# First pass: the first layer with its folded taps by high and low parts, each blended block split on POOL

## The chip, the cores and the metric

One core of one Trainium2 chip runs the whole kernel. The metric is the device time of one execution in microseconds; the time before is the median of three runs. TensorE is the matrix engine (PE in the rows, its weight loads PEld), VectorE is DVE, ScalarE is ACT, GpSimd is POOL, and SyncE (SP) issues most transfers.

## The reference

The input is x, 32 images of 56 x 56 positions with 96 channels, fp32. Four layers follow one another (L0 to L3). Only the first, L0, is touched here:

```python
x_norm = (x - mu) / sqrt(var + EPS) * gamma + beta
x_gray = x_norm.mean(-1)
grad_h = abs(x_gray[:, :, 1:] - x_gray[:, :, :-1]).mean(axis=(1, 2))
grad_v = abs(x_gray[:, 1:, :] - x_gray[:, :-1, :]).mean(axis=(1, 2))
scores = stack([grad_h, grad_v, 0.8 * (grad_h + grad_v) * 0.5, abs(grad_h - grad_v)], axis=1)
idx = argmax(softmax(relu(scores @ sel_w1 + sel_b1) @ sel_w2 + sel_b2), axis=-1) % 4
x_sel = where(idx == 1, swapaxes(x_norm, 1, 2), x_norm)
t = x_sel.reshape(b, h * w, c) @ fc1_w + fc1_b
t = depthwise_convolution_of_3_along_the_sequence(t, dw_w) + dw_b
out = gelu(t) @ fc2_w + fc2_b
return x + out
```

L1 to L3 are blocks of windowed attention with an MLP or a convolution; their code is the same before and after.

## The kernel before

`scan_pass` computes L0; three calls of `window_pass` compute L1 to L3 after it. In `scan_pass` an image lies in SBUF as 96 channels by 3136 positions, cut into NB = 7 blocks of TB = 448 positions. Each engine has its own program, written out by hand, and semaphores order them.

`step(i, norm, conv, turn)` runs three things side by side on each engine: normalising image i and deciding its flag (norm), the convolution and the second layer of image i - 1 (conv), and transposing image i + 1 (turn). `over_images` calls it for image 0, then in a loop for images 1 to 30, then for 31, and last for the convolutions of image 31 alone. A step has 14 slots k = 0 to 13, one for each half block: block m = k // 2, half h = k % 2 of the 192 hidden channels.

- TensorE. `conv_half` (L395) computes half a block of the first layer: the three taps of the convolution are folded into the weights `W1T`, so it is three fp32 matmuls of 97 rows, 96 columns of weights and 448 positions, on `XS` shifted by 0, 1 and 2 positions, added up in one bank. `fc2_block` (L407) is the second layer of a block, `mean` (L373) and `variance` (L379) serve the normalisation, `turn_block` (L359) transposes. The small matmuls of the decision stand ahead of their slots: score (L433, slot 9), sel1 (L436, slot 10), sel2 (L439, slot 11), flag (L442, slot 12). `conv_half` waits, at the first half of a block, until the blended blocks up to m + 1 are there (`xs`), and for the Gelu that frees its bank.
- ACT. Squares (L473), Ln and Exp for the reciprocal deviation (L481, L484), Gelu (L511). Gelu and Ln/Exp are in different table sets, so a table load stands between them.
- VectorE. Copies of the turned image out of PSUM (L531), centring copies `XM` (L565), the product `XN` (L570), the small operations of the decision (L584 to L612), the residual into `OUT` (L543, two instructions, which read the bank and `XM`), and the blend: for each block `XS = XN * (1 - flag)` (L620) and `XS = XN transposed * flag + XS` (L623). The blend stands in slots 12 (blocks 0 to 2) and 13 (blocks 3 to 6), with the residual of block 5 between them and that of block 6 behind, and then the centring copy of the next image.
- SP loads images and stores `OUT`. POOL has nothing to do in this pass.

`XS` has two buffers, taken in turn by images, and a row of ones for the bias (L258). The helper `split_weights` (L153, L157) is used for the later passes: on VectorE it makes `high = cast(whole)` in fp32r and `low = whole - high`. There, `by_parts` (L998) and `output` (L1090) compute a product as high x high + high x low + low x high with three fp32r matmuls, and POOL splits operands (L1473 and L1475, L1482 and L1484, L1535 and L1537).

Of the kernel before, what the change touches and what calls it, by code (L numbers as in the profile page):

```python
# [31 lines left out]
F32R = mybir.dt.float32r  # L32
# [157 lines left out]
def scan_pass(nc, PS, w, x, xa):  # L190
# [20 lines left out]
    with ExitStack() as ctx:  # L211
# [10 lines left out]
        XT = sb("XT", [112, TP, C]); X = sb("X", [C, S])  # L222
        XM = sb("XM", [GY, 2, S]); XN = sb("XN", [GY, S]); XS = sb("XS", [C + 1, 2, S + 2])
        SQ = sb("SQ", [C, 2, 2 * TB]); LV = sb("LV", [GY, 2, 2 * TB]); RS = sb("RS", [GY, 2, 2 * TB])
# [22 lines left out]
        with nc.Block() as block:  # L247
            @block.tensor
            def _(pe):
                pe.matmul(PS[0:C, 1, 0:1], J[:, 0:C], gcol[:, 0:1], start=True, stop=True).then_inc(gamma_mean, 1)  # L250

            @block.vector
            def _(dve):
                for t in range(3):
                    dve.tensor_tensor(W1T[0:C + 1, t, :], W1[0:C + 1, :], taps[0:C + 1, t, :], ALU.mult)

                for p in range(2):
                    dve.memset(XS[C:C + 1, p, 1:S + 1], 1.0)  # L258


                dve.tensor_tensor(CM[:, 0:C], ident[0:C, 0:C], J[:, 0:C], ALU.subtract)
                dve.wait_ge(gamma_mean, 1)
                dve.tensor_copy(gmean[:], PS[0:C, 1, 0:1]).then_inc(gamma_out, 1)
                dve.wait_ge(gamma_out, 1)
                dve.tensor_scalar(CM[:, C + 1:C + 2], gcol[:], gmean[:, 0:1], 1.0 / C, ALU.subtract, ALU.mult)

        s = {n: sem(n) for n in ("img_loaded", "turned", "x_ready", "mean", "xm", "sq", "var", "lv", "rstd",
                                 "xn", "grey_tiles", "diffs", "sums", "sums_ready", "score", "scores", "sel1", "hidden", "sel2",
                                 "dve_chain", "centred", "expo", "flag", "flagb", "flag_ready", "factors", "blend", "xs",
                                 "conv", "gelu", "fc2", "out")}  # L270
        stored, passed = [sem("stored0"), sem("stored1")], sem("passed")
# [28 lines left out]
        with nc.Block() as block:  # L300
# [49 lines left out]
            def _(pe):  # L350
# [30 lines left out]

                def conv_half(c, xs, k):

                    m, h = k // 2, k % 2
                    if h == 0:

                        pe.wait_ge(s["xs"], c * NB + min(m + 2, NB))
                    if k >= 3:
# [5 lines left out]
                    for t in range(3):  # L394
                        mm = pe.matmul(PS[0:C, 4 + k % 3, 0:TB], W1T[0:C + 1, t, h * C:(h + 1) * C],  # L395
                                       xs[:, m * TB + t:m * TB + t + TB], start=(t == 0), stop=(t == 2))
                    mm.then_inc(s["conv"], 1)
# [12 lines left out]
                def step(i, norm, conv, turn):  # L410
                    c = base(pe, i - 1)
                    i1 = base(pe, i + 1)
                    xs = pick(XS, parity(pe, c)) if conv else None
                    for k in range(SLOTS):
# [28 lines left out]
                        if conv:  # L443
                            conv_half(c, xs, k)
                            if k % 2 == 1 and k >= 3:
                                fc2_block(c, k // 2 - 1)
# [75 lines left out]
            def _(dve):  # L522
# [23 lines left out]
                def step(i, norm, conv, turn):  # L546
# [11 lines left out]
                    if norm:  # L558
                        p = parity(dve, i)
                        xm, xs = pick(XM, p), pick(XS, p)  # L560
                    old = pick(XM, parity(dve, c)) if conv else None

# [9 lines left out]
                    for k in range(SLOTS):  # L572
# [43 lines left out]
                        if norm and k >= FLAG:  # L616

                            for m in (range(NB // 2), range(NB // 2, NB))[k - FLAG]:
                                cols = slice(1 + m * TB, 1 + (m + 1) * TB)
# [11 lines left out]
                for m in range(NB):  # L631
                    copy_turned(0, m)
                over_images(dve, step)


# [1111 lines left out]
```

## Time and profile before

| | |
|---|---|
| time, median of 3 runs | 11815.78 us (11811.32 to 11822.69) |
| profiled execution, its own time | 11807.14 us |
| its span, first to last instruction | 11805.3 us |
| mean granted TensorE clock | 0.977 |
| PE busy | 11116.6 us (94%) |
| DVE busy | 7378.2 us (62%) |
| ACT busy | 7831.3 us (66%) |
| POOL busy | 5227.8 us (44%), none of it in the first pass |
| L395 PE, first layer of the first pass | 2688 records, 552 ns on average |

All times in the rows are from that one profiled execution. In the first pass one image follows another in the same pattern, so the rows of one image (from 1012 to 1077 us) stand for the pass. A fp32 matmul shows as two records of the matmul and two weight loads; an fp32r matmul shows as one of each. Matmul records overlap, so the distance between starts is what one costs.

### The profile page before, as it was taken

How to read it: one execution, taken by the hardware profiler on the slowest of the kernel's cores; microseconds unless marked ns; L12 is line 12 of the kernel's file. 1: busy time of each engine (PE TensorE's matmuls, PEld its weight loads, DVE VectorE, ACT ScalarE, POOL GpSimd, SP SyncE). 2: the span in 40 equal slices, each digit the busy share in tenths (PEclk: the TensorE clock that was granted, in tenths of full speed). 3: DMA queues.
4: the chain of work that ended last, by engine and by line, in shares of the span. 5: the costliest groups of instructions: out<-in, count | busy, mean ns of one | idle time of the engine just before them, and what ended most of it. 6: DMA issues, size and time to landing. Idle time of an engine off the chain costs nothing. (4 is left out here: it accounts for less than half of the span.)

```text
span 11805.3 us, 397033 instructions
## 1 busy us (share of the span) xinstructions
PE 11116.6 (94%) x158740; PEld 8317.4 (70%) x158740; DVE 7378.2 (62%) x12642; ACT 7831.3 (66%) x13524; POOL 5227.8 (44%) x6916
## 2 busy tenths in 40 slices
PE   6999999899999999998989999998999999999999
PEld 2444444577777777777767777776888888788887
DVE  4444444577777777775447777776666666666665
ACT  4555555477777777776337777775777777777776
POOL 0000000377777777775014544443555555555554
PEclk9999999899999999999989999998999999999999
DMA  1111111122222222222643333332010000010100
GB/s 54 39 40 36 40 35 40 33 53 50 52 51 51 51 52 51 51 51 77 216 146 80 81 79 79 80 79 54 24 25 24 25 24 24 25 25 25 24 24 22
DMA packets 1105622, 617.63 MB, mean 52 GB/s; under 512 B 864651, under 2 KB 1076566, under 8 KB 1099704
## 3 DMA queue, kind: packets, MB, share of 16 engines
q1 hardware_dynamic: 1091496, 553.66, 19.3%
q10 hardware_dynamic: 12288, 38.54, 1.0%
q8 instruction: 1265, 20.73, 0.8%
q14 instruction: 573, 4.69, 0.1%
HBM read 308.38 MB, written 282.75 MB: 50 GB/s over the span
## 5 line engine op out<-in xcount | busy, mean ns | idle before, releaser
L1484 POOL TENSOR_TENSOR L_HdL<-L_Hd,L_HdH 128x392 fp32r<-128x392 f32 x1536 | 1572.7, 1024 | 283.8 <-POOL L_HdH L1482 283.1
L1468 POOL TENSOR_TENSOR L_SQ<-L_X 96x392 f32<-96x392 f32 x512 | 428.5, 837 | 2298.8 <-DMA L_X<-after_L 2288.6
L991 PE MATMUL banks<-L_ident,L_PR 113*113 113x113 f32 x9216 | 1201.1, 267 | 1.2 <-DVE L_X L1390 0.7
L991 PEld LDWEIGHTS banks<-L_ident,L_PR 113*113 113x113 f32 x9216 | 1143.1, 180 | 63.8 <-DVE L_X L1390 9.8
L1219 ACT COPY L_PT<-banks 113x452 f32<-113x452 f32 x1792 | 885.8, 538 | 371.1 <-PE banks L991 369.2
L1235 ACT ACTIVATE L_PR<-L_SX 113x588 f32<-113x588 f32 x1536 | 1088.0, 708 | 52.3 <-DVE L_SX L1362 10.3
L1482 POOL CAST L_HdH<-L_Hd 128x392 fp32r<-128x392 f32 x1536 | 785.1, 511 | 740.5 <-issue 658.1
L395 PE MATMUL banks<-scan_XS,scan_W1T 97*96 (+1 forms) x2688 | 1111.4, 552 | 0.0
L1054 PE MATMUL banks<-L_VB,L_PT 113*49 113x34 f32 x36864 | 1064.1, 213 | 2.0 <-ACT L_PT L1219 1.0
L1262 ACT ACT_TABLE_LOAD x512 | 656.9, 1283 | 607.3 <-PE banks L998 607.2
L1356 DVE TENSOR_REDUCE L_MX<-banks 113x12 f32<-113x588 f32 x1024 | 783.4, 765 | 432.2 <-PE banks L1037 432.2
L1054 PEld LDWEIGHTS banks<-L_VB,L_PT 113*49 113x49 f32 x36864 | 1016.1, 126 | 25.4 <-issue 2.5
L1473 POOL CAST L_XNH<-L_XN 97x392 fp32r<-97x392 f32 x512 | 447.6, 874 | 1155.4 <-DVE L_XN L1403 1155.4
L1362 DVE TENSOR_TENSOR L_SX<-banks,L_MX 113x588 f32<-113x588 f32 x1024 | 788.9, 770 | 35.3
L395 PEld LDWEIGHTS banks<-scan_XS,scan_W1T 97*96 97x96 f32 x2688 | 434.0, 167 | 514.9 <-issue 510.6
L1037 PEld LDWEIGHTS banks<-L_KX,L_QT 32*49 32x49 f32 x36864 | 562.6, 118 | 310.0 <-issue 307.9
L1037 PE MATMUL banks<-L_KX,L_QT 32*49 32x98 f32 x36864 | 720.3, 248 | 28.9 <-issue 28.0
L1090 PE MATMUL banks<-L_HdH,L_W2H 128*97 128x392 f32 x1536 | 611.1, 398 | 130.4 <-POOL L_HdL L1484 130.2
L1013 PE MATMUL banks<-L_Wv,L_XN 97*49 97x48 f32 x24576 | 730.2, 213 | 0.0
L1532 POOL COPY L_XN<-L_XR 96x392 f32<-96x392 f32 x256 | 147.9, 578 | 1276.5 <-DMA L_XR<-L_norm 1270.7
L1371 DVE COPY L_PT<-banks 113x452 f32<-113x452 f32 x512 | 321.9, 629 | 617.9 <-PE banks L991 617.9
L1072 PE MATMUL banks<-L_OT,L_Wp 97*97 97x392 f32 x1536 | 691.9, 532 | 2.8 <-ACT L_OT L1265 1.1
(239 smaller groups left out, 27006.6 us busy)
## 6 DMA issues: line engine op xcount, KB each, us to landing
L_X<-after_L SPq DMA_DIRECT2D x768, 147.0 KB
after_L<-L_X SPq DMA_DIRECT2D x512, 147.0 KB
conv_T<-L_norm_by_phase SPq DMA_DIRECT2D x96, 512.0 KB, 3.3
L_norm_by_phase<-L_XP SPq DMA_DIRECT2D x512, 84.0 KB, 2.1
scan_XT<-in_x SPq DMA_DIRECT2D x33, 1176.0 KB, 7.1
L_norm<-L_XA SPq DMA_DIRECT2D x256, 147.0 KB, 1.9
L_conv<-conv_D ACTq DMA_DIRECT2D x96, 392.0 KB, 3.0
L_XR<-L_norm SPq DMA_DIRECT2D x256, 147.0 KB, 2.6
```

The lines of the kernel that those rows point to most:

```text
L395: mm = pe.matmul(PS[0:C, 4 + k % 3, 0:TB], W1T[0:C + 1, t, h * C:(h + 1) * C], xs[:, m * TB + t:m * TB + t + TB], start=(t == 0), stop=(t ...
L991: mm = pe.transpose(bank(TURN[a])[0:SPAN, (k % 4) * SPAN:(k % 4 + 1) * SPAN], PR[:, st.v if lag else st.u, 2 * k:2 * k + 2, :].rearrange(" ...
L1013: mm = pe.matmul(bank(VALUES_BANK)[HALF * e:HALF * e + TOK, q * G * HD:(q + 1) * G * HD], XN[:, st.u, q * TOK:(q + 1) * TOK], Wv[0:C + 1, ...
L1037: mm = pe.matmul(bank(g)[p0:p0 + TOK, q // 2 * 2 * TOK:(q // 2 + 1) * 2 * TOK].rearrange("c (e k) -> c e k", e=2), QT[rows, st.u, q * TOK: ...
L1054: mm = pe.matmul(bank(HEADS_BANK)[p0:p0 + TOK, col:col + VW], PT[:, st.v, q // 2 * G + g, p0:p0 + TOK], VB[:, st.v, q, g, :], start=True, ...
L1072: pe.matmul(bank(PROJ_BANK)[0:C + 1, 0:CH], Wp[0:C + 1, :], OT[:, st.v], start=mlp, stop=True).then_inc(s["proj"], 1)
L1219: act.copy(PT[:, st.v if lag else st.u, 4 * a:4 * a + 4, :].rearrange("c k q -> c (k q)"), bank(TURN[a])[0:SPAN, 0:4 * SPAN]).then_inc(s[f ...
L1235: act.activation(PR[:, u, a, 0:TOK], SX[:, u, a], ACT.Exp).then_inc(s[f"probs{half}"], 1)
L1356: dve.tensor_reduce(mx, src, AX.X, ALU.max).then_inc(s[f"rowmax{half}"], 1)
L1362: dve.tensor_tensor(dst, src, spread, ALU.subtract).then_inc(s[f"centred{half}"], 1)
L1482: pool.tensor_copy(HdH[:, u, j].bitcast(F32R), Hd[:, u, j]).then_inc(s[f"hd_high_{j}"], 1)
L1484: pool.tensor_tensor(HdL[:, u, j].bitcast(F32R), Hd[:, u, j], HdH[:, u, j], ALU.subtract).then_inc(s[f"hd_parts_{j}"], 1)
```

## The change

The first layer of the first pass is computed by high and low parts. `W1T` is split once into `W1TH` and `W1TL` with `split_weights`, which also splits the prepared `XS` (zero edges, row of ones) into both buffers of `XSH` and `XSL`. For each image VectorE blends into a single buffer `XS`; POOL casts each blended block to fp32r (`XSH`) and subtracts (`XSL`), and raises `xs_parts`, for which `conv_half` now waits. `conv_half` issues nine fp32r matmuls in place of three fp32 ones. VectorE waits for `xs_parts` of the image before ahead of the first blend.

```diff
-        XM = sb("XM", [GY, 2, S]); XN = sb("XN", [GY, S]); XS = sb("XS", [C + 1, 2, S + 2])
+        XM = sb("XM", [GY, 2, S]); XN = sb("XN", [GY, S]); XS = sb("XS", [C + 1, S + 2])
+        XSH = sb("XSH", [C + 1, 2, S + 2]); XSL = sb("XSL", [C + 1, 2, S + 2])
+        W1TH = sb("W1TH", [128, 3, 2 * C]); W1TL = sb("W1TL", [128, 3, 2 * C])
...
-                for p in range(2):
-                    dve.memset(XS[C:C + 1, p, 1:S + 1], 1.0)
+                dve.memset(XS[C:C + 1, 1:S + 1], 1.0)
...
+        split_weights(nc, "scan_parts", [(W1T[0:C + 1], W1TH[0:C + 1], W1TL[0:C + 1])]
+                      + [(XS[:], XSH[:, p], XSL[:, p]) for p in range(2)])
...
-                def conv_half(c, xs, k):
+                def conv_half(c, xh, xl, k):
...
-                        pe.wait_ge(s["xs"], c * NB + min(m + 2, NB))
+                        pe.wait_ge(s["xs_parts"], c * NB + min(m + 2, NB))
...
-                        mm = pe.matmul(PS[0:C, 4 + k % 3, 0:TB], W1T[0:C + 1, t, h * C:(h + 1) * C],
-                                       xs[:, m * TB + t:m * TB + t + TB], start=(t == 0), stop=(t == 2))
+                        for n, (wt, xt) in enumerate(((W1TH, xh), (W1TH, xl), (W1TL, xh))):
+                            mm = pe.matmul(PS[0:C, 4 + k % 3, 0:TB], wt[0:C + 1, t, h * C:(h + 1) * C].bitcast(F32R),
+                                           xt[:, m * TB + t:m * TB + t + TB].bitcast(F32R), start=(t == 0 and n == 0), stop=(t == 2 and n == 2))
...
+                            if k == FLAG and (not isinstance(i, int) or i >= 1):
+                                dve.wait_ge(s["xs_parts"], i * NB)
...
+            @block.gpsimd
+            def _(pool):
+                def step(i, norm, conv, turn):
+                    if not norm:
+                        return
+                    p = parity(pool, i)
+                    xh, xl = pick(XSH, p), pick(XSL, p)
+                    for m in range(NB):
+                        cols = slice(1 + m * TB, 1 + (m + 1) * TB)
+                        hold(pool, s["xs"], i * NB + (m + 1), passed)
+                        pool.tensor_copy(xh[0:C, cols].bitcast(F32R), XS[0:C, cols]).then_inc(s["xs_high"], 1)
+                        hold(pool, s["xs_high"], i * NB + (m + 1), passed)
+                        pool.tensor_tensor(xl[0:C, cols].bitcast(F32R), XS[0:C, cols], xh[0:C, cols], ALU.subtract).then_inc(s["xs_parts"], 1)
+
+                over_images(pool, step)
```

## Rows read from the trace of the kernel before

**Rows 1.** The page, its first line: the span.

```profile
span 11805.3 us, 397033 instructions
```

**Rows 2.** Busy us of PE, PEld, DVE, ACT, POOL in a stretch; clock, DMA.

```profile
1056.00:1060.00 4.00, 4.00 (x15) 2.38 (x13) 3.82 (x7) 1.55 (x2) 0.00 (x0) 0.57 0.20 50
```

**Rows 3.** Timeline of PE, one image: start us, us, line, tiles, [idle <- releaser].

```profile
1012.68 4.75 PE L395 MATMUL banks<-scan_XS,scan_W1T 97*96 x12
1017.27 1.67 PE L407 MATMUL banks<-scan_Hd,scan_W 96*97 96x448 f32 x4
...
1029.90 1.75 PE L379 MATMUL banks<-scan_SQ,scan_J 96*98 96x448 f32 x4 [0.54 <-ACT scan_SQ L473]
...
1055.15 2.27 PE L359 MATMUL banks<-scan_ident,scan_XT 112*96 112x112 f32 x16 [1.69 <-ACT scan_LV L481]
1057.22 3.60 PE L395 MATMUL banks<-scan_XS,scan_W1T 97*96 x6
...
1066.27 0.18 PE L433 MATMUL banks<-scan_gone,scan_GA 56*4 56x1 f32 x2 [0.53 <-issue]
...
1072.91 0.19 PE L439 MATMUL banks<-scan_sw,scan_hid 16*1 16x4 f32 x2
...
1076.96 0.33 PE L442 MATMUL banks<-scan_fl,scan_one 1*96 1x2 f32 x2
```

**Rows 4.** Timeline of DVE, the same image.

```profile
1013.76 0.45 DVE L620 TENSOR_SCALAR scan_XS<-scan_XN,scan_fb 96x448 f32 x1 [0.16 <-DVE scan_fb L612]
...
1015.21 0.45 DVE L620 TENSOR_SCALAR scan_XS<-scan_XN,scan_fb 96x448 f32 x1
...
1019.17 0.81 DVE L543 SCALAR_TENSOR_TENSOR scan_OUT<-banks,scan_fc2b,scan_XM 97x424 f32<-97x424 f32 x2 [0.98 <-PE banks L407]
...
1024.69 1.04 DVE L623 SCALAR_TENSOR_TENSOR scan_XS<-scan_XN,scan_fb,scan_XS 96x448 f32 x1
...
1076.51 0.14 DVE L609 TENSOR_SCALAR scan_fl<-scan_fl 1x1 f32<-1x1 f32 x1
```

**Rows 5.** Timeline of ACT, the same image.

```profile
1027.60 1.28 ACT L473 ACT_TABLE_LOAD   x1 [9.51 <-DVE scan_XM L565]
```

**Rows 6.** Timeline of PE in the second pass: fp32r matmuls in a row.

```profile
3011.22 0.34 PE L998 MATMUL banks<-L_XNH,L_WqH 97*96 97x392 f32 x1
...
3011.40 0.34 PE L998 MATMUL banks<-L_XNL,L_WqH 97*96 97x392 f32 x1
```

**Rows 7.** Timeline of DVE and POOL in the second pass.

```profile
3005.73 0.57 DVE L1407 TENSOR_TENSOR L_XN2L<-L_XN,L_XN2H 97x392 fp32r<-97x392 f32 x1
3005.79 0.88 POOL L1473 CAST L_XNH<-L_XN 97x392 fp32r<-97x392 f32 x1 [1.17 <-DVE L_XN L1403]
```

**Rows 8.** Third pass, DVE and POOL: timeline, then groups (count, busy us, mean ns, idle).

```profile
6520.86 0.51 POOL L1535 CAST L_XNH<-L_XN 97x392 fp32r<-97x392 f32 x1 [0.17 <-POOL L_XN L1532]
6520.90 1.09 DVE L1362 TENSOR_TENSOR L_SX<-L_SR,L_MX 113x588 f32<-113x588 f32 x1
...
6521.55 1.32 POOL L1537 TENSOR_TENSOR L_XNL<-L_XN,L_XNH 97x392 fp32r<-97x392 f32 x1 [0.18 <-POOL L_XNH L1535]
...
L1545 POOL TENSOR_TENSOR L_DWL<-L_DW,L_DWH 96x392 fp32r<-96x392 f32 x256 | 260.3, 1017 | 46.1 <-POOL L_DWH L1543 46.1
...
L1362 DVE TENSOR_TENSOR L_SX<-banks,L_MX 113x588 f32<-113x588 f32 x1024 | 788.9, 770 | 35.3
```

**Rows 9.** Timeline of DVE while constants and weights are prepared.

```profile
56.05 2.67 DVE L258 MEMSET scan_XS<- 1x3136 f32 x1 [0.69 <-issue]
...
2188.38 0.21 DVE L153 CAST L_WqH<-L_Wq 97x96 fp32r<-97x96 f32 x1 [0.64 <-PEq L73]
...
2188.62 0.35 DVE L153 CAST L_W1H<-L_W 97x384 fp32r<-97x384 f32 x1
...
2189.23 0.26 DVE L157 TENSOR_TENSOR L_WqL<-L_Wq,L_WqH 97x96 fp32r<-97x96 f32 x1
...
2189.57 0.55 DVE L157 TENSOR_TENSOR L_W1L<-L_W,L_W1H 97x384 fp32r<-97x384 f32 x1
```

More of the change, by code:

```diff
@@ L269, in scan_pass @@
                                  "dve_chain", "centred", "expo", "flag", "flagb", "flag_ready", "factors", "blend", "xs",
-                                 "conv", "gelu", "fc2", "out")}
+                                 "xs_high", "xs_parts", "conv", "gelu", "fc2", "out")}
         stored, passed = [sem("stored0"), sem("stored1")], sem("passed")
@@ L412, in step @@
                     i1 = base(pe, i + 1)
-                    xs = pick(XS, parity(pe, c)) if conv else None
+                    if conv:
+                        p = parity(pe, c)
+                        xh, xl = pick(XSH, p), pick(XSL, p)
                     for k in range(SLOTS):
@@ L443, in step @@
                         if conv:
-                            conv_half(c, xs, k)
+                            conv_half(c, xh, xl, k)
                             if k % 2 == 1 and k >= 3:
@@ L559, in step @@
                         p = parity(dve, i)
-                        xm, xs = pick(XM, p), pick(XS, p)
+                        xm, xs = pick(XM, p), XS
                     old = pick(XM, parity(dve, c)) if conv else None
@@ L633, in _ @@
                 over_images(dve, step)
+            @block.gpsimd
[4 more added lines that the diff above has]
+                    p = parity(pool, i)
+                    xh, xl = pick(XSH, p), pick(XSL, p)
+                    for m in range(NB):
[5 more added lines that the diff above has]
+                over_images(pool, step)
 class Step:
```

## The prediction

> **What bounds the kernel now.** The page gives the profiled execution a span of 11805.3 us [rows 1]. The change touches the first pass alone. A busy share, 94% of the span for TensorE, is no bound, so I followed one image through the timeline of each engine, from L395 of slot 12 at 1012.68, which stands right behind the flag matmul, to the next flag matmul at 1076.96: 64.3 us, 64.5 with the flag matmul itself [rows 3]. It falls into four parts, and TensorE sets the end of only some.
>
> - S1, flag to the ACT table load ahead of the square (1027.60) [rows 5]. VectorE sets it: seven blends, the residual of block 5, the residual of block 6 and the centring copy. Its one wait is 0.98 us, for the second layer's matmuls [rows 4]; ACT then waited 9.51 us for that copy [rows 5], and TensorE 0.54 us for the square (L379) [rows 3].
> - S2, from there to the transposes at 1055.15: a chain of table loads, squares, Ln and Exp on ACT with the copies of VectorE in it. TensorE waits for it, 1.69 us at the transposes [rows 3]; convolutions 2 to 6 lie beside it.
> - S3, transposes to score matmul (1066.27): TensorE until the second layer of block 2, then VectorE's residual, its three copies L531 and the sums; at the score TensorE had idled 0.53 us [rows 3].
> - S4, score to flag: TensorE back to back; behind sel2 (1072.91) a parallel chain of softmax pieces whose last part L609 ends at 1076.65 [rows 4], 0.31 us ahead of the flag matmul.
>
> **The matmuls.** Half a block was 3 fp32 matmuls, 6 records; the 12 records of two halves take 4.59 us from 1012.68 to the next row's start at 1017.27, the first of them a little longer: 2.25 us a half, 0.375 a record [rows 3]. It becomes 9 fp32r matmuls. The nearest rows step 0.18 us at 392 columns [rows 6]; scaled by columns a step is between 0.195 (only the 56 extra columns at the rate of the fp32 pass, 0.375 / 448 / 2 each) and 0.21. I take 0.20, and 0.07 for the first of a group: 1.87 us, so 0.38 less a half. If the extra address arithmetic of 9 instructions showed, it would be near 2.1 and the saving 0.15; nothing below the 9 steps is possible.
>
> What that brings by part, without POOL. S1: two halves precede the residual that VectorE awaits, but its own blends end 0.98 us before: -0.76. S2: zero, ACT's chain covers it; if ACT were not there it would be 5 x 0.38. S3: convolution 7 runs partly at the lower clock level: its six records take 3.60 us, not 2.42, and the stretch 1056 to 1060 has a granted clock of 0.57, so most of it is at 1.2 instead of 2.4 GHz [rows 2, 3], behind a wait of 1.69 us and the transposes. The slow stretch is a stretch of time: in it an fp32 record steps 0.75, an fp32r one 0.375 (448 columns at half the rate), so it costs both about half its length. The gain stays near 0.38, a little more as a step of 0.20 less than doubles: -0.43. Convolution 8 gains nothing, the three copies are late next. S4: convolutions 9 and 10 give 0.38 each; for 11 the softmax chain is late next, so only 0.15: -0.91. Sum: -2.10 us an image.
>
> **The splits on POOL.** Each blended block now gets a cast and a subtraction on POOL, 96x448. Nearest rows: cast 0.51 us (L1535) and subtraction 1.02 (L1545) for 392 columns [rows 8]; scaled, 0.56 and 1.15, with a step of some 0.18 us between them and ahead of each. That is 2.0 us a block against VectorE's 1.45 (1013.76 to 1015.21) [rows 4]. POOL idles in this pass, and TensorE needs only two blocks' parts before convolution 0, ten microseconds later, so POOL's own time is hidden. VectorE's new wait (the parts of the image before) is long satisfied and costs nothing; queued behind it would be the blends.
>
> What is not hidden is the use of SBUF by both. In the second pass a POOL cast that met VectorE's subtraction with two SBUF inputs (L1407) took 0.88 us, not 0.51: it ended 0.37 us after VectorE's [rows 7]. In the third pass VectorE's L1362, SBUF inputs both, started 0.04 us after a POOL cast and took 1.09 us where the same shape takes 0.77: it ended 0.62 us after the cast. POOL's next operation then met L1362 and took 1.32 instead of 1.02 [rows 8]. So such operations exclude each other whole. L623 has two SBUF inputs (XN and XS). L620 has one, but moves 448 elements in 0.45 us: less than the 1.0 ns an element of a two-input operation (0.26 us at 96, 0.55 at 384, L157) and in line with the cast's 0.49 ns (0.21 and 0.35, L153) [rows 4, 9]: it uses two read paths, and no row shows such an operation against POOL.
>
> The Trainium skill, "SBUF — State Buffer", section "SBUF: two separate sides", says of the pair shared by VectorE and GpSimd that it is held by whichever starts first, for the whole instruction, and that a two-port mode takes it as well as two SBUF inputs. By that L620 excludes POOL too, and the sum would be the upper of the two below, 11918 us.
>
> Worked through from L620 at 1013.76, where a blocked operation runs its own time less 0.14 after the other's end (the L1362 and L1537 rows): L620 0.31, L623 0.91, cast 0.42, subtraction 1.00. If POOL is served at every hand-over, a block costs VectorE 0.31 + 0.42 + 0.91 + 1.00 = 2.64 us; the first two are freer, and the last blend ends at 1030.2, where it ended at 1025.7: +4.5. If VectorE keeps the pair from L623 to the next L620, POOL enters only in the gap ahead of L623, alternately with a cast and a subtraction: 1028.9, +3.2. The 0.98 us of waiting is used up in both. I take +3.8 between these ends, because the rows don't tell the order at a hand-over. This replaces S1's -0.76. Outside these ends lies the case without exclusion, a rival below.
>
> **The rest.** Setup: a new block before the loop, on VectorE and in series. Casts: 0.44 + 2 x 1.7; subtractions: 0.74 + 2 x 3.3 by the slopes above for 576 and 3138 columns; the barrier ahead of such a block 0.64 (the idle time before the first cast [rows 9]) and about as much behind it: 12.4. Off goes one memset of ones, 2.67 + 0.60 [rows 9]: +9.1. The smaller first memset lies under the loads. The last step has convolutions alone, TensorE back to back: 14 x 0.38 = -5.3.
>
> **Sum.** 31 x (3.8 - 0.91) = +89.6; 30 x (-0.43) = -12.9; +9.1 - 5.3: +80.5 us. On the span of 11805.3 us that is 11885.8; the execution's own time is 1.8 more than its span (11807.14), and the median of the runs, 11815.78, is 8.6 more than that: 11896.
>
> **The rivals.**
> - Exclusion at its two ends (both in my forecast): +3.2 gives 11878, +4.5 gives 11918.
> - L620 doesn't exclude POOL. Then POOL gets in under it and L623 waits only for the rest: the last blend ends at 1026.1, +0.35. 31 x (0.35 - 0.91) - 12.9 + 3.8 = -26: 11789. For it: no row shows a one-input operation blocked. Against: its rate of two elements in the time of one.
> - No exclusion: 31 x (-0.76 - 0.91) - 12.9 + 3.8 = -61: 11755, faster. It decides if the rows of the passes with POOL were due to something else; three kinds of row say otherwise.
> - More idle, lower clock: TensorE now waits 5 to 6 us for the square in each image where it waited 0.54. If the clock falls there, variance 0 ends up to 1.7 us later; ACT reads it only behind two table loads (1.28 us each [rows 5]), two Gelus and a square, so that is free; but a second fall over convolutions 9 to 11 would add 1 to 2 us an image, beside the exclusion: 11927 to 11958.
> - The splits' parts arrive late for the convolutions: POOL would have to need over 5 us a block (convolution time of a block with its second layer); at 2.6 it doesn't decide.
>
> **How the numbers follow.** Exclusion, either order, 0.66: 11855 to 11935 with the matmul step and the clock of convolution 7 open. Worse (clock, or POOL slower than its rows) 0.10. Partial exclusion 0.13. None 0.11. About 0.2%, 24 us, is what a measurement of this kernel can tell. Partial exclusion spreads over both sides of that line, half and half. Faster 0.18, same 0.08, slower 0.74. The range takes in the partial case at 11775 and part of the worse one to 11942; the forecast's own range is 11855 to 11935.
>
> **What would show each step.** L395: nine fp32r records a half, step 0.20. L623 and L620: means over 1.05 and 0.45, L623 near 1.3 to 1.9; POOL's casts over 0.56. From flag to the table load about 19 us, from the table load to the transposes 27.5 as before; L379 waiting about 5 us for the square; score to flag 9.8. If L620 and L623 keep their means, the prediction is wrong and the time falls under 11800; if the step of L395 is 0.24 or more, the gains of S3 and S4 vanish and it goes to 11925 or over.

## The result and the profile after

| | before | after |
|---|---|---|
| median of the runs (15 each), us | 11814.59 | 11844.65 |
| ratio, 95% interval | 1 | 1.0026 (1.0017 to 1.0034) |
| the profiled execution, us | 11807.14 | 11852.66 |
| its span, us | 11805.3 | 11850.9 |

The change makes the kernel 30 us slower by the medians; the two profiled executions are 45.6 us apart by their spans. Two of the 15 runs of after, 12341 and 12827 us at a granted clock of 0.80 and 0.75 where the others have 0.97, stay out of the ratio; without them the median of after is 11842.77 us. Here are the span and the busy times on the page of after, to be held against [rows 1]:

```profile
span 11850.9 us, 401791 instructions
PE 11020.4 (93%) x160084; PEld 8592.4 (73%) x160084; DVE 7502.6 (63%) x12647; ACT 7843.1 (66%) x13524; POOL 5678.7 (48%) x7364
```

TensorE is less busy than before and the kernel is slower: the busy share was no bound. The first thing to do is to cut both spans at the memset of the PSUM banks that opens each pass. The cut gives, in us:

| pass | before | after | difference |
|---|---|---|---|
| 1 (changed) | 2164.4 | 2222.3 | +57.9 |
| 2 | 3923.4 | 3903.8 | -19.6 |
| 3 | 2083.0 | 2085.0 | +2.0 |
| 4 | 3634.5 | 3639.7 | +5.2 |

Passes 2 to 4 compute the same by the same code, and the second is 20 us shorter. The forecast had nothing there.

The first pass, by the parts of the prediction, as means over the 24 images between the 6th and the 30th flag (us; the first two columns count from the flag matmul). The table counts S1 to the square itself; the prediction counted it to the table load ahead of the square, which starts 1.29 us earlier in both kernels, so the differences are the same:

| | last blend ends | square starts (S1) | square to transposes (S2) | transposes to score (S3) | score to flag (S4) | flag to flag |
|---|---|---|---|---|---|---|
| before | 13.32 | 16.48 | 26.25 | 10.77 | 10.67 | 64.17 |
| after | 15.72 | 18.88 | 26.28 | 10.79 | 9.68 | 65.63 |
| difference | +2.40 | +2.40 | +0.03 | +0.02 | -0.99 | +1.46 |

Now the lines. Timeline of DVE of after, blocks of the blend (start, us, engine, line, operation, out<-in); [rows 4] are the same work before:

```profile
1046.60 0.45 DVE L628 TENSOR_SCALAR scan_XS<-scan_XN,scan_fb 96x448 f32<-96x448 f32 x1
...
1048.55 1.25 DVE L631 SCALAR_TENSOR_TENSOR scan_XS<-scan_XN,scan_fb,scan_XS 96x448 f32<-96x448 f32 x1
...
1058.12 1.17 DVE L631 SCALAR_TENSOR_TENSOR scan_XS<-scan_XN,scan_fb,scan_XS 96x448 f32<-96x448 f32 x1
1059.21 1.27 DVE L628 TENSOR_SCALAR scan_XS<-scan_XN,scan_fb 96x448 f32<-96x448 f32 x1
1060.52 1.14 DVE L631 SCALAR_TENSOR_TENSOR scan_XS<-scan_XN,scan_fb,scan_XS 96x448 f32<-96x448 f32 x1
```

The same stretch on POOL; the bracket is the idle time before a line and who ended it:

```profile
1048.47 0.56 POOL L653 CAST scan_XSH<-scan_XS 96x448 f32 x1 [50.12 <-DVE scan_XS L631]
...
1058.75 1.49 POOL L655 TENSOR_TENSOR scan_XSL<-scan_XS,scan_XSH 96x448 f32 x1 [0.24 <-POOL scan_XSH L653]
1060.18 0.72 POOL L653 CAST scan_XSH<-scan_XS 96x448 f32 x1
...
1062.58 0.56 POOL L653 CAST scan_XSH<-scan_XS 96x448 f32 x1
```

Read the ends. L631 ends at 1059.29. The subtraction, which POOL had begun at 1058.75, ends at 1060.24, 0.95 us later, so it did most of its work behind L631. L628, begun at 1059.21, ends at 1060.48, 0.24 us behind the subtraction: alone it takes 0.45 (the line at 1046.60), here 1.27. The cast begun at 1060.18 ends at 1060.90, 0.42 us behind L628. L631, begun at 1060.52 with 0.38 us of the cast to go, ends at 1061.66, 0.76 us behind the cast. So each waits for the other's end, as the forecast had it, and a block takes 0.95 + 0.24 + 0.42 + 0.76 = 2.37 us, where it took 1.45.

The last of the four waits is easily overlooked, because L631 grows by only 0.10 us, from 1.04 to 1.14. It is a wait all the same. The cast begun at 1048.47 ends at 1049.03; L631, begun at 1048.55 with 0.48 us of it to go, takes 1.25 and ends at 1049.80, 0.77 us behind it. Between 200 and 2000 us there are 165 such meetings of L631 with a cast, and it ends 0.75 to 0.79 us behind the cast in all of them, 0.77 in the mean. L631 grows by what is left of the cast when it starts, less 0.28 us.

This is one image of two kinds. In every second image, which uses the other of the two buffers, the subtraction takes 1.31 us and not 1.47, and a block 2.21 us; the mean of the blocks from the third on is 2.30. POOL's operations grow too, the cast from 0.56 to 0.72 us and the subtraction from 1.13 (0.97 in the other buffer): that is the same exclusion seen from the other side.

What follows from the late copy is in the waits of TensorE, 1000 to 1900 us (what waited, for what: us in total, times, longest), first before, then after:

```profile
PE banks L359 <- ACT scan_LV L481: 23.6, 14, 1.7
PE banks L379 <- ACT scan_SQ L473: 20.4, 28, 0.9
```

```profile
PE banks L382 <- ACT scan_SQ L479: 57.9, 28, 4.4
PE banks L362 <- ACT scan_LV L487: 35.8, 14, 2.6
```

L382 (was L379) now waits up to 4.4 us for the square, since the matmuls are shorter and the square later. Those are the idle microseconds that the fp32r matmuls freed; they are not on the path.

### The profile page after: what moved, and what is told of

Read it like the earlier page. It is cut to its first block and busy times, and to the rows that moved or that the text cites. A ratio compares the mean times of both kernels' runs of the same rounds, so it can differ in the third digit from the quotient of the medians.

```text
span 11850.9 us, 401791 instructions
## 1 busy us (share of the span) xinstructions
PE 11020.4 (93%) x160084; PEld 8592.4 (73%) x160084; DVE 7502.6 (63%) x12647; ACT 7843.1 (66%) x13524; POOL 5678.7 (48%) x7364
## 5 line engine op out<-in xcount | busy, mean ns | idle before, releaser
L653 POOL CAST scan_XSH<-scan_XS 96x448 f32 (+1 forms) x224 | 151.0, 674 | 1680.8 <-DVE scan_XS L631 1680.8
L1096 PE MATMUL banks<-L_OT,L_Wp 97*97 97x392 f32 x1536 | 691.3, 532 | 2.9 <-ACT L_OT L1289 1.1
L1037 PEld LDWEIGHTS banks<-L_Wv,L_XN 97*49 97x49 f32 x24576 | 634.6, 127 | 78.2 <-issue 2.9
```

The lines of the kernel that those rows point to most:

```text
L1037: mm = pe.matmul(bank(VALUES_BANK)[HALF * e:HALF * e + TOK, q * G * HD:(q + 1) * G * HD], XN[:, st.u, q * TOK:(q + 1) * TOK], Wv[0:C + 1, ...
L1096: pe.matmul(bank(PROJ_BANK)[0:C + 1, 0:CH], Wp[0:C + 1, :], OT[:, st.v], start=mlp, stop=True).then_inc(s["proj"], 1)
```

## The experiments

Each of the first eight was run 5 times, the subtraction alone and the first filled kernel 11 times; ratios are to the kernel before, run beside it on the same chip (medians 11817.58 us for the first four, 11814.99 for the next four). Edits are against the kernel after, where nothing else is said.

**1. The matmuls alone.** No program for POOL in the pass, the first layer reads parts that nobody renews:

```diff
-            @block.gpsimd
-            def _(pool):
-                ...
-                            if k == FLAG and (not isinstance(i, int) or i >= 1):
-                                dve.wait_ge(s["xs_parts"], i * NB)
```

> The nine fp32r matmuls and the setup of the changed kernel, POOL idle in the first pass; the convolution waits for the blends and reads parts that are not renewed (the splits of the images are left out). Theory, exclusion between POOL's splits and the blends: L623's successor keeps 1.05 us, flag to square falls by 0.76 from 16.5 us, score to flag by 0.99; transposes to score between -0.4 and 0. Setup +8, end -6. Sum 52 to 66 us under the kernel before: 11750 to 11763. Rival, the low clock or the nine matmuls themselves take the gain: at or over 11800.

11741.8 us, ratio 0.9942 (0.9929 to 0.9956). In the table's terms: square at 15.67 (-0.81), transposes to score 10.60 (-0.17), score to flag 9.68 (-0.99), flag to flag 62.21. So the terms -0.76 and -0.91 of the matmuls hold, S3's -0.43 doesn't. The time is 8 us under what was expected (11750 to 11763): the first pass is 59.3 us under before, inside the expected 52 to 66, but the second pass is 19.6 us shorter here too, as in after. Against after, the splits cost 3.42 us an image, 3.21 of them before the square.

**2. The splits alone.** The kernel before with its fp32 matmuls, and POOL splitting each block into parts that nobody reads:

```diff
+            @block.gpsimd
+            def _(pool):
+                ...
+                        pool.tensor_copy(xh[0:C, cols].bitcast(F32R), xs[0:C, cols]).then_inc(s["xs_high"], 1)
+                        hold(pool, s["xs_high"], i * NB + (m + 1), passed)
+                        pool.tensor_tensor(xl[0:C, cols].bitcast(F32R), xs[0:C, cols], xh[0:C, cols], ALU.subtract).then_inc(s["xs_parts"], 1)
```

> The kernel before with its fp32 matmuls on two buffers of XS, and POOL's cast and subtraction of every block beside them, read by nobody. Exclusion: the stretch from the start of the first blend to the end of the last grows by 2.75 us as in the changed kernel, 31 images: +85, 11900. Rival, the loss came from waiting for the parts: nobody waits for them here, so within 10 us of the kernel before.

11877.69 us, ratio 1.0054 (1.0041 to 1.0068). The square starts at 19.62, 3.14 later than before: the cost of the splits is there with matmuls of either kind, and TensorE waits for no part here. The total is less than expected because transposes to score took 9.43 us, 1.34 less: convolution 7 had 2.26 us in every image, its length at full clock, where before it had 2.95 in the mean. The stretches at 1.2 GHz fell elsewhere.

**3 and 4. The cast alone, the subtraction alone.**

```diff
-                        pool.tensor_copy(xh[0:C, cols].bitcast(F32R), XS[0:C, cols]).then_inc(s["xs_high"], 1)
-                        hold(pool, s["xs_high"], i * NB + (m + 1), passed)
-                        pool.tensor_tensor(xl[0:C, cols].bitcast(F32R), XS[0:C, cols], xh[0:C, cols], ALU.subtract).then_inc(s["xs_parts"], 1)
+                        pool.tensor_copy(xh[0:C, cols].bitcast(F32R), XS[0:C, cols]).then_inc(s["xs_parts"], 1)
```

> The changed kernel without POOL's subtraction (the low parts are not renewed), POOL casts alone. If a cast is nearly free beside L623 (0.12 us in the trace of the changed kernel): at most 10 us over the run without splits, about 11765. If it costs its own 0.42 us as the prediction had it: 2.5 us an image less 0.2 of slack, 11825.

```diff
-                        pool.tensor_copy(xh[0:C, cols].bitcast(F32R), XS[0:C, cols]).then_inc(s["xs_high"], 1)
-                        hold(pool, s["xs_high"], i * NB + (m + 1), passed)
```

> The changed kernel without POOL's cast (the low parts are the difference to high parts that are not renewed). If the subtraction carries the exclusion, 0.94 us a block of the 0.93 that a block grew: 0 to 10 us under the changed kernel, 11835 to 11845. If both operations share the cost as predicted (1.00 and 0.42): 30 to 40 us under it, about 11810.

The cast alone: 11758.03 us, ratio 0.9954 (0.9940 to 0.9967), 16 us over experiment 1 where at most 10 were expected; the square at 16.01, 0.34 behind experiment 1, is worth 10.5 of them, and transposes to score, 0.21 longer, another 6. The subtraction alone: 11841.19, ratio 1.0023 (1.0013 to 1.0032), square at 18.91, 3.24 behind it, and within 0.03 of after, which has both. The groups of the blend (count, busy us, mean ns, idle time), between 1000 and 1900 us; the cast alone:

```profile
L631 DVE SCALAR_TENSOR_TENSOR scan_XS<-scan_XN,scan_fb,scan_XS 96x448 f32<-96x448 f32 x105 | 122.1, 1163 | 3.7
L653 POOL CAST scan_XSH<-scan_XS 96x448 f32 x105 | 58.7, 559 | 883.3 <-DVE scan_XS L631 883.3
L628 DVE TENSOR_SCALAR scan_XS<-scan_XN,scan_fb 96x448 f32<-96x448 f32 x105 | 46.4, 442 | 2.0
```

The subtraction alone:

```profile
L631 DVE SCALAR_TENSOR_TENSOR scan_XS<-scan_XN,scan_fb,scan_XS 96x448 f32<-96x448 f32 x98 | 149.3, 1524 | 3.5
L653 POOL TENSOR_TENSOR scan_XSL<-scan_XS,scan_XSH 96x448 f32 x97 | 102.4, 1056 | 806.5 <-DVE scan_XS L631 806.5
L628 DVE TENSOR_SCALAR scan_XS<-scan_XN,scan_fb 96x448 f32<-96x448 f32 x98 | 50.1, 511 | 1.8
```

After, both:

```profile
L655 POOL TENSOR_TENSOR scan_XSL<-scan_XS,scan_XSH 96x448 f32 x91 | 122.7, 1348 | 22.2 <-POOL scan_XSH L653 22.2
L631 DVE SCALAR_TENSOR_TENSOR scan_XS<-scan_XN,scan_fb,scan_XS 96x448 f32<-96x448 f32 x93 | 106.9, 1149 | 3.3
L628 DVE TENSOR_SCALAR scan_XS<-scan_XN,scan_fb 96x448 f32<-96x448 f32 x93 | 81.3, 874 | 1.8
...
L653 POOL CAST scan_XSH<-scan_XS 96x448 f32 x92 | 61.8, 672 | 699.2 <-DVE scan_XS L631 699.2
```

Without splits L631 has a mean of 1059 ns and L628 one of 444 (experiment 1). The cast adds 0.10 us to L631 in the mean and nothing to L628, far less than the 0.42 a block by which experiment 3 was to judge the forecast. Yet it is awaited here too. POOL and DVE with the cast alone:

```profile
1067.74 0.56 POOL L653 CAST scan_XSH<-scan_XS 96x448 f32 x1 [53.09 <-DVE scan_XS L631]
1069.32 0.56 POOL L653 CAST scan_XSH<-scan_XS 96x448 f32 x1 [1.02 <-DVE scan_XS L631]
```

```profile
1067.74 1.33 DVE L631 SCALAR_TENSOR_TENSOR scan_XS<-scan_XN,scan_fb,scan_XS 96x448 f32<-96x448 f32 x1
1069.46 1.18 DVE L631 SCALAR_TENSOR_TENSOR scan_XS<-scan_XN,scan_fb,scan_XS 96x448 f32<-96x448 f32 x1
```

With 0.56 us of the cast to go L631 takes 1.33, with 0.42 to go 1.18; it ends 0.77 and 0.76 us behind the cast. The subtraction alone, POOL and DVE:

```profile
1049.73 1.13 POOL L653 TENSOR_TENSOR scan_XSL<-scan_XS,scan_XSH 96x448 f32 x1 [1.60 <-DVE scan_XS L631]
```

```profile
1049.85 1.78 DVE L631 SCALAR_TENSOR_TENSOR scan_XS<-scan_XN,scan_fb,scan_XS 96x448 f32<-96x448 f32 x1
```

L631 ends at 1051.63, again 0.77 us behind POOL. So both operations are awaited whole, and what differs is how much of them is left when VectorE's next operation starts: little of a cast, most of a subtraction. The prices don't add up for this reason. With the subtraction alone a block takes 2.09 us in the mean from the third on, 0.2 less than with both, but the second block takes 2.16 (1.65 with both) and the one with the residual 2.65 (2.31 with both), and the blend is as long: 14.74 us against 14.71.

**5. The splits late.** Both operations stay, but from block 2 on POOL begins when the last block is blended; only blocks 0 and 1, which convolution 0 needs, are split at once:

```diff
-                        hold(pool, s["xs"], i * NB + (m + 1), passed)
+                        hold(pool, s["xs"], i * NB + (m + 1 if m < 2 else NB), passed)
```

> The changed kernel, but POOL splits only blocks 0 and 1 beside the blends; from block 2 on it waits for the last blend of the image. Theory, the subtraction beside the blends is the cost, 3.2 us an image for six of them: two of them left cost 1.1 to 1.9, and the two idle microseconds of VectorE take part of it. Flag to square 16.2 to 17.0 us against 18.9, period down by 1.9 to 2.7, so 11845 - 58 to 84: 11761 to 11787. Rival, the parts come late for the convolutions: TensorE waits at convolution 2 and the time stays at 11845 or above.

11737.13 us, ratio 0.9934 (0.9921 to 0.9948): 78 us under before, 108 under after. POOL in this kernel, first inside the blend, then behind it:

```profile
1001.55 1.48 POOL L655 TENSOR_TENSOR scan_XSL<-scan_XS,scan_XSH 96x448 f32 x1 [0.24 <-POOL scan_XSH L653]
...
1011.31 0.56 POOL L653 CAST scan_XSH<-scan_XS 96x448 f32 x1 [5.92 <-DVE scan_XS L631]
1012.11 1.14 POOL L655 TENSOR_TENSOR scan_XSL<-scan_XS,scan_XSH 96x448 f32 x1 [0.24 <-POOL scan_XSH L653]
```

The five blocks behind the blend are split at 0.56 and 1.14 us, unhindered, while VectorE is past its blends and ACT squares. The square starts at 16.28, 2.60 earlier than in after, flag to flag is 62.02. The splits' work is the same; only what it met has changed. The time is 24 us under what was expected (11761 to 11787). The square is where it was to be; what came on top is the stretch from transposes to score, 9.79 us instead of 10.79, 30 us in all. Of 26 waits ahead of the transposes, as long as in after (2.5 us in the mean), only 8 are followed by a slow stretch (21 of 25 in after). This was not expected, and what spares the other images is not shown.

The rival of late parts is refuted: although block 2's split waits 5.92 us longer and the others follow it, no wait of TensorE for them stands among its waits. That flag to flag is 0.2 us shorter than with no splits at all (62.02 against 62.21) is the clock's doing: 0.61 more before the square, 0.81 less from transposes to score.

**6. Late, and a leaner setup.** Experiment 5, and the row of ones and the split of `XS` made beside the loads of the weights; behind them only the split of `W1T`. A new argument of the loading helper does it on VectorE:

```diff
-                dve.memset(XS[C:C + 1, 1:S + 1], 1.0)
-        split_weights(nc, "scan_parts", [(W1T[0:C + 1], W1TH[0:C + 1], W1TL[0:C + 1])]
-                      + [(XS[:], XSH[:, p], XSL[:, p]) for p in range(2)])
+        split_weights(nc, "scan_parts", [(W1T[0:C + 1], W1TH[0:C + 1], W1TL[0:C + 1])])
```

> The same, and the splits of the prepared XS moved ahead, beside the loads of the weights. The trace of the changed kernel has the first transposes 8.4 us later than before; with it they should come at 68 to 70 us, so 8 to 10 us under the run before this one. If the loads were not what the start waits for, no gain.

11733.13 us, ratio 0.9931 (0.9917 to 0.9944), the fastest here. The large casts and subtractions, in after and then in this kernel (DVE):

```profile
59.52 3.49 DVE L153 CAST scan_XSH<-scan_XS 97x3138 fp32r<-97x3138 f32 x2
63.72 6.76 DVE L157 TENSOR_TENSOR scan_XSL<-scan_XS,scan_XSH 97x3138 fp32r<-97x3138 f32 x2
```

```profile
41.29 3.50 DVE L187 CAST scan_XSH<-scan_XS 97x3138 fp32r<-97x3138 f32 x2
44.82 6.76 DVE L190 TENSOR_TENSOR scan_XSL<-scan_XS,scan_XSH 97x3138 fp32r<-97x3138 f32 x2
```

The first transposes start at 68.1 us, not at 78.7 as in experiment 5. The first pass is 16.7 us shorter in its trace (2094.3 against 2111.0), but the fourth is 11.9 longer (3649.1 against 3637.2), and the medians differ by 4, where 8 to 10 were expected. Of the 11.9 us, 4.8 lie between the first two projections of the pass (16.2 us apart instead of 11.5) and 3 at the restarts of its loop; why is open.

**7 and 8. The wait filled.** Is it the wait of TensorE ahead of the transposes after which the clock falls? Eight fp32r matmuls on constants, into a bank that is free at that point, go in front of it:

```diff
+                                if conv:
+                                    pe.wait_ge(s["gelu"], c * SLOTS + 5)
+                                    for f in range(8):
+                                        pe.matmul(PS[0:C, 5, 0:TB], W1TH[0:C + 1, 0, 0:C].bitcast(F32R),
+                                                  W1TH[0:C + 1].rearrange("c t n -> c (t n)")[:, 0:TB].bitcast(F32R), start=True, stop=True)
```

> The changed kernel with eight matmuls of no use ahead of TensorE's wait before the transposes (bank 5, constants, 1.6 us in a wait of 2.6). Theory, the gain of convolution 7 is lost to a granted clock of 1.2 GHz behind that wait: with the wait filled the drops over transposes, convolution 7 and the second layer go, transposes to score falls from 10.8 to 9.1 us, 30 images: 11795. If the low clock there comes from the transposes and not from the wait: unchanged, 11845, or some microseconds worse.

Transposes to score fell from 10.79 to 9.08 us, as expected, and the first pass from 2222.3 to 2165.8. PE around the transposes, in after:

```profile
1025.28 2.22 PE L362 MATMUL banks<-scan_ident,scan_XT 112*96 112x112 f32 x16 [2.58 <-ACT scan_LV L487]
1027.17 0.69 PE L399 MATMUL banks<-scan_XSH,scan_W1TH 97*96 x1
...
1028.41 0.58 PE L399 MATMUL banks<-scan_XSH,scan_W1TH 97*96 x1
1028.79 0.58 PE L399 MATMUL banks<-scan_XSL,scan_W1TH 97*96 x1
```

And with the wait filled (L429 is the filling):

```profile
998.70 1.78 PE L429 MATMUL banks<-scan_W1TH 97*96 97x448 f32 x8
1001.44 1.73 PE L362 MATMUL banks<-scan_ident,scan_XT 112*96 112x112 f32 x16 [0.96 <-ACT scan_LV L492]
...
1003.62 0.36 PE L399 MATMUL banks<-scan_XSH,scan_W1TH 97*96 x1
1003.82 0.36 PE L399 MATMUL banks<-scan_XSL,scan_W1TH 97*96 x1
```

A step between two rows is 0.37 to 0.38 us in the first and 0.20 in the second. The same shows in the windows of 6 us from the transposes on (stretch, length, busy time of PE, PEld, DVE, ACT and POOL, each with its instructions, then the granted clock, the DMA share and GB/s), after and then filled:

```profile
1025.00:1031.00 6.00, 5.72 (x27) 4.63 (x28) 4.21 (x7) 3.18 (x6) 0.00 (x0) 0.72 0.14 33
```

```profile
1001.00:1007.00 6.00, 5.56 (x36) 4.31 (x37) 4.47 (x8) 3.99 (x9) 0.00 (x0) 1.00 0.14 33
```

Yet the time was 11825.88 us, ratio 1.0009 (1.0000 to 1.0018), where 11795 had been expected. Of 56 us in the first pass 30 are left by the traces, for the fourth pass, whose code is the same, took 3669.2 us instead of 3639.7; by the medians 19 are left. The same filling on top of experiment 6:

> All three together: the late splits, the early preparation and the filled wait. If the three are independent, 11845 less their gains: 11705 to 11740. If the fill does nothing: as the run of late splits with the early preparation.

11737.31 us, ratio 0.9935 (0.9921 to 0.9949). First pass 2086.2 us, the shortest of all, flag to flag 61.46; fourth pass 3664.3. No gain over experiment 6: the first pass is 8.1 us shorter than there, the fourth 15.2 longer.

**9 to 12. Padding.** What moves the passes that nobody changed? A first theory follows from which kernels agree: the second pass takes 3923 and 3928 us in before and in experiment 2, whose programs of TensorE are the same, and 3898 to 3905 in all the others; the fourth is long, by some 30 us, only in the two kernels with the filling. So it would be where TensorE's code lies. Four kernels test it, one execution each: the kernel before with N matmuls of one column in the setup of the first pass, for N = 16, 32, 64 and 128.

```diff
+                for f in range(16):
+                    pe.matmul(PS[0:C, 3, 0:1], J[:, 0:C], gcol[:, 0:1], start=True, stop=True)
```

> The kernel before with 16 one-column matmuls of no use added to TensorE's program in the preparation of the first pass. In the changed kernel the second pass, whose code is the same, took 3904 us and not 3923, all of it where its loop starts again (18.2 us a round trip and not 20.3). Theory, where TensorE's code lies sets what a loop costs at its start: with more instructions ahead of it the second pass changes by up to 20 us, the fourth by up to 30, at one or more of the four sizes, with nothing else changed. Rival, it comes from the first pass itself (buffers, timing): 3923 and 3635 us at every size.

> The same with 32 matmuls. Theory: the second pass between 3898 and 3928 us, not the same at all sizes. Rival: 3923 and 3635 us.

> The same with 64 matmuls, about as many instructions as the nine matmuls of the changed kernel add to the program (42 written halves with 6 more each). Theory: the second pass near 3904 us. Rival: 3923.

> The same with 128 matmuls. Theory: the second or the fourth pass off 3923 and 3635 us by over 5. Rival: the same as before.

| us | total | pass 1 | pass 2 | pass 3 | pass 4 |
|---|---|---|---|---|---|
| before (its first trace) | 11807.14 | 2164.4 | 3923.4 | 2083.0 | 3634.5 |
| 16 | 11793.29 | 2167.6 | 3902.1 | 2087.1 | 3634.6 |
| 32 | 11817.77 | 2165.0 | 3902.5 | 2106.3 | 3642.1 |
| 64 | 11827.61 | 2176.1 | 3924.2 | 2084.5 | 3641.1 |
| 128 | 11850.83 | 2197.5 | 3923.8 | 2086.7 | 3641.1 |

Before took 11803.78 beside them. For N = 64 and 128 the padding costs time of its own in the first pass: the first transposes come at 82.9 and 103.1 us, not at 70.0. Behind it, sixteen useless matmuls take 21 us off the second pass, 32 add 23 to the third, 64 put the second back (it was expected near 3904). The rival, 3923 and 3635 us at every size, is refuted.

The difference lies at one place, where the loop of a pass starts again. PE in the second pass of before, from the last projection of one turn (L1072; L1096 and L1074 are the same line) to the first of the next:

```profile
2989.48 0.90 PE L1072 MATMUL banks<-L_OT,L_Wp 97*97 97x392 f32 x2
...
2993.98 0.63 PE L998 MATMUL banks<-L_XNH,L_WkH 97*96 97x392 f32 x1 [3.60 <-issue]
...
2997.22 0.49 PE L998 MATMUL banks<-L_XNL,L_WqH 97*96 97x392 f32 x1 [1.63 <-issue]
...
3009.91 0.90 PE L1072 MATMUL banks<-L_OT,L_Wp 97*97 97x392 f32 x2
```

In after:

```profile
3045.67 0.90 PE L1096 MATMUL banks<-L_OT,L_Wp 97*97 97x392 f32 x2
...
3050.43 0.62 PE L1022 MATMUL banks<-L_XNH,L_WkH 97*96 97x392 f32 x1 [3.86 <-issue]
...
3063.40 0.90 PE L1096 MATMUL banks<-L_OT,L_Wp 97*97 97x392 f32 x2
```

With 16 padding matmuls:

```profile
2990.39 0.90 PE L1074 MATMUL banks<-L_OT,L_Wp 97*97 97x392 f32 x2
...
3007.75 0.90 PE L1074 MATMUL banks<-L_OT,L_Wp 97*97 97x392 f32 x2
```

Inside a turn two chunks are 12.6 us apart in all three; across the restart it is 20.4, 17.7 and 17.4. There are 9 restarts in the pass, with means of 20.4 us before and 18.3 after: 9 x 2.1 = 19 us, the whole difference of the pass. In the fourth pass they take 17.9 us in before and 21.3 and 21.1 in the two filled kernels: 9 x 3.3 = 30 us.

The rows show what a dear restart has and a cheap one lacks. At every restart TensorE stands for some 3 to 4 us, waiting for nothing that the profile shows ("issue"). In before it stands once more after the next four matmuls, for 1.63 us, in the middle of six matmuls of which the others follow one another without a gap, and the clock stays low for longer (0.73 over the 19 us from 2990, against 0.90 over the 17 us from 3046 in after). This second stop, of 1.1 to 2.7 us, is there at all 9 restarts of the second pass in before, in experiment 2 and with 64 and 128 padding matmuls, of the third pass with 32, and of the fourth pass in the two filled kernels, and at none of the other restarts of the 14 kernels. So it belongs to the program and not to chance, although each padded kernel ran only once.

## Why the prediction was off

The direction was right, and the time lies in the range, but it is not in the forecast's own range of 11855 to 11935, and the forecast of 80 us more is over twice the 30 measured. The step that failed is the size of one term of the sum, S1, the time until the square: +3.8 us an image were taken, +2.40 measured. The traces can be set against the sum, which was made against one profiled execution (45.6 us apart by the spans):

| term | forecast | measured | miss, us |
|---|---|---|---|
| S1, 31 times | +3.8 | +2.40 | -43.4 |
| S2, 31 times | 0 | +0.03 | +0.9 |
| S3, 30 times | -0.43 | +0.02 | +13.5 |
| S4, 31 times | -0.91 | -0.99 | -2.5 |
| setup (first transposes 70.0 to 78.4) | +9.1 | +8.4 | -0.7 |
| last step (last flag to the end of the pass, 68.4 to 62.6) | -5.3 | -5.8 | -0.5 |
| passes 2 to 4 | 0 | -12.4 | -12.4 |
| first and last images, as the rest | 0 | +10.2 | +10.2 |

The sum of the misses is -34.9, and 80.5 - 34.9 = 45.6. From the spans to the medians another 15 us go: the profiled execution of before lies 7.5 us under its median and that of after 8.0 above its own. Where a run of either kernel loses or gains those was not looked into, for only profiled runs have traces.

**S1, the term that was mis-sized.** The mechanism was right: the instructions exclude each other whole, L628 (was L620) with its one SBUF input too, and POOL is served at each hand-over. For that order the prediction had 0.31 + 0.42 + 0.91 + 1.00 = 2.64 us a block and +4.5 an image; measured were 2.37 in one kind of image, 2.30 in the mean, and +2.40. The 2.1 us between have three parts:

- What a blocked operation still takes behind the other's end. The prediction took its own time less 0.14 for all, from two rows of other operations [rows 8]. The 0.42 of the cast held (0.42), but L631 ends 0.76 behind the cast and not 0.91, L628 0.24 behind the subtraction and not 0.31, the subtraction 0.95 behind L631 and not 1.00. That is 0.27 a block, 1.4 us over the five blocks that meet POOL in full.
- In every second image the subtraction is 0.16 us shorter (0.97 against 1.13 without VectorE in its way): 0.4 us an image in the mean. Both buffers have the same shape, in experiment 2 both take 1.13, and why one is quicker here is open.
- 0.34 us ahead of the first blend: from the flag it takes 1.00 us, where it took 1.34. The residual of block 4 is out of the way by then, because the matmuls are shorter. The prediction took the matmuls' gain as used up by the exclusion, and this part was not.

The 0.14 stood in both ends of the range of S1, +4.5 and +3.2, so both missed. The order at a hand-over was the one of the upper end; that +3.8, taken between the ends, came nearer than +4.5 was luck.

The Trainium skill, "SBUF — State Buffer", section "SBUF: two separate sides", says that the pair is held by whichever starts first for the whole instruction, and that a two-port mode takes it as well as two SBUF inputs. The trace agrees for both operations of the blend: L628 takes 1.27 us instead of 0.45 and ends 0.24 us behind the subtraction, and L631 ends 0.77 us behind the POOL operation that it meets, a cast or a subtraction, however much of it was left.

The rivals without exclusion, and that with L620 free, are refuted by the same lines. The price of the exclusion in this kernel is 3.21 us before the square in each image (after against experiment 1), 100 us over 31 images: more than the 76 us that the matmuls alone bring (experiment 1).

**S3.** The matmuls of convolution 7 did become shorter, by 0.34 us in the mean (2.95 to 2.61), against 0.43 forecast. At full clock the stretch from transposes to score is 9.43 us with fp32 matmuls (experiment 2) and 9.08 with fp32r ones (experiment 7), -0.35. What failed is the step that the slow stretch costs both about the same. It was 1.34 us before and 1.71 in after: the wait ahead of the transposes went from 1.69 us [rows 3] to 2.58, and the first pass has 70 stretches at 1.2 GHz where it had 27, with a granted clock of 0.93 between 200 and 2000 us, not 0.98. The rival "more idle, lower clock" named this and put its cost on convolutions 9 to 11. It came on the transposes and convolution 7; the slow stretches behind the wait for the square cost nothing, as that rival said (S2 has +0.03). That the wait belongs to it is shown by experiments 7 and 8, which fill it and lose the slow stretch in every image. The wait alone doesn't decide: in experiment 5 it is as long, and most images stay at full clock. Experiment 2, at full clock through convolution 7, fits: there TensorE waited for this in 9 images, at most 1.5 us, where before had 14 waits and the longest of 1.7. How long such a wait must be was not measured.

**Last image.** From the 31st to the 32nd flag it took 65.46 us, where it took 56.26 before and 59.68 with the subtraction alone. TensorE waited there at the score,

```profile
2142.69 0.18 PE L439 MATMUL banks<-scan_gone,scan_GA 56*4 56x1 f32 x2 [3.14 <-DVE scan_GA L597]
```

and ran at 1.2 GHz for the next 17 us. This is one place in one execution, about 6 of the 45 us, and most of the last row of the table.

**Passes 2 to 4.** The prediction took unchanged code as unchanged time. Here the second pass alone is worth 20 us. By the first pass alone the change costs 57.9 us; a third of that came back from something that has nothing to do with splitting. Experiment 5 has the same gift in it: its 78 us under before are 53 from the first pass and 20 from the second. The padded kernels show that instructions added ahead in TensorE's program are enough to switch it, and that its price is a second stop of TensorE at the loop's restart. That it is the place of the code, and the fetching of instructions at a jump back, is the obvious reading, but not shown.

**What held.** The step of 0.20 us and 1.87 for half a block (1.89 in the rows of experiment 7); the gains of S1 without POOL (-0.81 for -0.76) and of S4; nothing in S2; setup and last step within a microsecond. The signs that it named came: L628 and L631 grew over 0.45 and 1.05, score to flag 9.7 for 9.8. From the flag of 1045.60 to the table load it was 17.9 us, not 19, and that is S1's miss:

```profile
1063.53 1.28 ACT L479 ACT_TABLE_LOAD   x1 [13.15 <-DVE scan_XM L571]
```

## What to carry to other kernels

Work that is given to an idle POOL is not free while VectorE streams from SBUF: splitting all blocks under the blend put 3.2 us on the path in each image, and with five of the seven held back until the blend was over it was 0.6 (square at 16.28 against 15.67 without splits). So ask of such a step not only whether POOL has the time, but what VectorE runs meanwhile and which of the two the path goes through; and let POOL hold back what isn't needed at once. When a few tenths of a per cent are at stake, cut both traces by pass before explaining anything: code that nobody changed moved here by 20 to 30 us, as much as the whole change, and a kernel with a few padding instructions is a fair control. And when two engines exclude each other, read the distance between the ends of their instructions, not only how much one has grown: an instruction can wait for another and grow by a tenth of a microsecond.

## What the runs showed of the hardware that was not expected

- A number of instructions added far ahead in TensorE's program changes what a restart of a later loop costs by 2 to 3 us, 20 to 30 us a pass (3902 or 3923 us for the second, 2085 or 2106 for the third, 3635 or 3669 for the fourth). A dear restart has a second stop of TensorE, of 1.1 to 2.7 us, shortly behind the first; it is there at all 9 restarts of a pass or at none.
- A two-input operation of VectorE (96x448, 1.05 us alone) ends 0.77 us behind the POOL cast or subtraction that it meets, a one-input operation (0.45 us alone) 0.25 us behind a subtraction. So a cast of 0.56 us can cost it 0.10 or 0.28 us, by how much of it is left.
- A subtraction of 96x448 on POOL takes 1.13 us into one of two like buffers and 0.97 into the other, undisturbed (experiment 5).
- Eight useless matmuls, 1.78 us in a wait of 2.6, kept TensorE at 2.4 GHz and made the stretch behind them 1.7 us shorter.
